# Routing of the first six batches inside the attention, fixed slot columns for each expert, and tables that pick the processed columns

## What is computed

```python
x = x + _L0_xattn_ref(_layernorm(x), ctx_2048, w_qkv, w_proj, b_proj)
x = x + _L0_ffn_ref(_layernorm(x), conf_w, conf_b, gate_w, up_w, down_w, wealth)
# _L0_ffn_ref, with x the normed rows:
confidences = jax.nn.sigmoid(jnp.einsum('bsh,eh->bse', x, conf_w) + conf_b)
bids = confidences * wealth
top_bids, selected_experts = jax.lax.top_k(bids, 2)
routing_weights = jax.nn.softmax(top_bids, axis=-1)
# per expert: down(silu(gate(x)) * up(x)), summed with the two weights
```

## Time and profile before

| | us |
|---|---|
| median of 3 runs (lowest to highest) | 543.18 (542.64 to 545.73) |
| the profiled execution's own time | 545.19 |
| its span, first to last instruction | 543.6 |

### The profile page before, as it was taken

One profiled execution on the slowest core, in us unless ns is written; L12 is line 12 of the kernel. 1 busy time (PEld: TensorE's weight loads), 2 busy tenths in 40 slices (PEclk: granted clock), 3 DMA queues, 4 the chain that ended last, 5 costly groups with the idle time before them and its releaser, 6 DMA issues. The chain is left out here.

```text
span 543.6 us, 10607 instructions
## 1 busy us (share of the span) xinstructions
PE 468.6 (86%) x3467; PEld 283.5 (52%) x3468; DVE 356.5 (66%) x646; ACT 290.1 (53%) x584; POOL 181.4 (33%) x381
## 2 busy tenths in 40 slices
PE   2489999999999999999999984736699999999930
PEld 1245555555555555555555532735266666666620
DVE  7798797887887987978898805478133333333317
ACT  2237877777877878777788783210033333333310
POOL 6141222412312313223101001014356766677630
PEclk9759999999999999999999998555599999999985
DMA  6512223343342333331212002500101111111126
GB/s 178 126 41 66 67 81 112 78 114 98 84 128 74 99 111 81 86 88 40 75 39 76 2 2 69 164 0 0 25 25 45 39 39 40 39 41 41 39 72 181
DMA packets 32254, 38.10 MB, mean 70 GB/s; under 512 B 5604, under 2 KB 20580, under 8 KB 32212
## 3 DMA queue, kind: packets, MB, share of 16 engines
q1 hardware_dynamic: 27252, 30.79, 21.0%
q0 software_dynamic: 2560, 5.25, 3.8%
q10 hardware_dynamic: 2400, 1.51, 1.0%
HBM read 16.58 MB, written 4.72 MB: 39 GB/s over the span
## 5 line engine op out<-in xcount | busy, mean ns | idle before, releaser
L463 DVE TENSOR_REDUCE max_part<-max_ps 128x2 f32<-128x1024 f32 (+1 forms) x192 | 225.9, 1220 | 38.5 <-PE max_ps L561 30.6
L422 ACT ACTIVATE probs<-ring_ps 128x512 f32<-128x512 f32 x384 | 198.4, 604 | 50.1 <-PE ring_ps L584 47.0
L584 PE MATMUL ring_ps<-blocks,keys 64*128 64x512 f32 x384 | 151.1, 471 | 2.1 <-ACT probs L422 1.7
L594 PE MATMUL pv_ps<-probs,value_cols 128*32 128x256 f32 x1536 | 103.4, 387 | 0.0
L561 PE MATMUL max_ps<-keys,blocks 64*128 64x512 f32 x256 | 84.6, 449 | 7.6 <-DMA blocks<-masked 6.5
L1018 DVE TENSOR_TENSOR hidden<-up_ps,silu 128x512 f32<-128x512 f32 x40 | 27.7, 692 | 84.1 <-PE up_ps L1108 81.9
L584 PEld LDWEIGHTS ring_ps<-blocks,keys 64*128 64x128 f32 x384 | 65.3, 186 | 31.9 <-ACT probs L422 25.5
L911 ACT ACTIVATE hiddenT<-at_ps 128x512 f32<-128x512 f32 x40 | 23.9, 597 | 75.7 <-PE at_ps L1125 67.2
L338 POOL CAST maxes<-rowmax 128x8 fp32r<-128x8 f32 x32 | 6.3, 197 | 170.3 <-DVE rowmax L470 170.3
L594 PEld LDWEIGHTS pv_ps<-probs,value_cols 128*32 128x32 f32 x1536 | 40.4, 109 | 40.3 <-issue 14.6
L561 PEld LDWEIGHTS max_ps<-keys,blocks 64*128 64x128 f32 x256 | 42.4, 196 | 26.8 <-issue 16.7
(11 more groups left out here) (148 smaller groups left out, 465.2 us busy)
## 6 DMA issues: line engine op xcount, KB each, us to landing
keys<-parts SPq DMA_DIRECT2D x96, 96.0 KB
blocks<-masked SPq DMA_DIRECT2D x93, 64.0 KB
ctx_v_sb<-ctx_v_dram SPq DMA_DIRECT2D x8, 256.0 KB, 2.9
gate<-gateT_dram SPq DMA_DIRECT2D x8, 256.0 KB, 2.9
up<-upT_dram SPq DMA_DIRECT2D x8, 256.0 KB, 2.9
y_in<-pick_outs SPq DMA_DIRECT2D x8, 256.0 KB, 5.0
raw<-ctx_kT_dram SPq DMA_DIRECT2D x7, 256.0 KB, 2.7
h_rows<-h SPq DMA_DIRECT2D x4, 256.0 KB, 5.2
```

Of the source, the lines that this page charges most:

```text
L422: act.activation(probs[par][:, k, PAIR * a:PAIR * (a + 1)], bank("exp", s * XUNITS + u)[:].rearrange("p (g n) -> p g n", n=N), ACT.Exp).th ...
L463: vec.reduce_max(out, bank, axis=AX.X).then_inc(max_done, 1)
L584: pe.matmul(ps[:], keys[rows, t, k * P:(k + 1) * P], blocks[rows, t], start=True, stop=True)\
L594: mm = pe.matmul(pv_ps[ROWS * g:ROWS * (g + 1), 0:N], value_cols[:, t, k, g, :], probs[q % 2][:, k, g, :], start=(k == 0), stop=(k == KT - 1))
```

## The change

**Within the attention.** DVE takes the statistics of batch b-1 in step r = 1 of batch b (`row_statistics`). POOL norms its rows in r = 2 (`norm_rows`, with a power instead of a root), SP stores them to DRAM in r = 3, and POOL forms the logits of one tile in each of the steps r = 0 and r = 1 of the next batch (`logits`: one product of 128 x 1024 and a tree of seven additions). So twelve tiles (EARLY) have logits by step 30. In step 30 DVE forms bids and ranks of these twelve (`early_bids`, `rank_tiles`), PE counts (`count_tiles`), and in steps 31 to 33 DVE computes their places and one-hot matrices (now 128 wide on both sides) in portions of 14, 5 and 5, and PE multiplies them in portions of 8 (`find`). POOL forms the logits of tiles 12 and 13 in the last steps.

**After the barrier.** Norms and logits are left for the last two tiles, ranks, places and one-hot matrices for the last four.

**Fixed columns.** Expert e owns the slot columns 16e to 16e+15, so a place needs no count of the other experts. Which 40 of the columns are processed stands in two tables that POOL computes, `table` (the expert) and `columns`. In the loop POOL reads the column number with a load into a register before each copy. The number of slots stays 40. `max_ps` (attention), `gate_ps` and `up_ps` (experts) share the PSUM tensors `wide`.

```diff
+EARLY = QT * (B - 2)
+REACH = TILES
+LAST = QUADS - 1
+HOT_TURNS = (0, 14, 19, 2 * EARLY)
...
+def rank_tiles(vec, r, lo, hi, pair, pair2):
...
+    pairs = [P, n, E, E]
+    this, other = bids.unsqueeze(3).to_broadcast(pairs), bids.unsqueeze(2).to_broadcast(pairs)
+    vec.tensor_tensor(pair2, other, this, ALU.is_gt)
+    then(vec.tensor_tensor(pair, other, this, ALU.is_equal))
+    then(vec.tensor_tensor(pair, pair, r.earlier[:].unsqueeze(1).to_broadcast(pairs), ALU.mult))
+    then(vec.tensor_tensor(pair, pair, pair2, ALU.add))
+    then(vec.tensor_reduce(rank, pair, axis=AX.X, op=ALU.add))
+    vec.tensor_scalar(r.picks[:, lo:hi, :], rank, 1.5, None, ALU.is_lt).then_inc(r.picks_ready, 1)
+    for k in range(2):
+        op = vec.tensor_scalar(top[:, k], rank, float(k), None, ALU.is_equal)
+    then(op)
+    for k in range(2):
+        op = vec.tensor_tensor(picked[:, k], top[:, k], bids, ALU.mult)
+    then(op)
+    then(vec.tensor_reduce(best[:, :, :, 0], picked, axis=AX.X, op=ALU.add))
+    for k in range(2):
+        vec.tensor_tensor(r.gap[:, k, lo:hi], best[:, k], best[:, 1 - k], ALU.subtract).then_inc(r.gap_ready, 1)
...
+def place_tiles(vec, r, lo, hi, ps, base):
...
+    n = hi - lo
+    place, top, picked = r.place[:, lo:hi], r.top[:, :, lo:hi], r.picked[:, :, lo:hi]
+    then(vec.tensor_tensor(place, ps[:, 0:n * E].rearrange("p (t e) -> p t e", e=E),
+                           base[:].unsqueeze(1).to_broadcast([P, n, E]), ALU.add))
+    for k in range(2):
+        op = vec.tensor_tensor(picked[:, k], top[:, k], place, ALU.mult)
+    then(op)
...
+def hot_pick(vec, r, k, t, lane_hot, slot_hot):
+
+    vec.tensor_scalar(lane_hot, r.index[:], r.lane[:, k, t:t + 1], r.pick_id[:, k * TILES + t:k * TILES + t + 1],
+                      ALU.is_equal, ALU.mult)
+    vec.tensor_scalar(slot_hot, r.index[:], r.slot[:, k, t:t + 1], None, ALU.is_equal).then_inc(r.hot_ready, 1)
...
+def count_tiles(pe, r, lo, hi, ps):
+
+    n = hi - lo
+    pe.matmul(ps[:, 0:(n + 1) * E], r.before_r[:], r.picks[:, lo:hi + 1].rearrange("p t e -> p (t e)"), start=True, stop=False)
+    for t in range(n):
+        mm = pe.matmul(ps[:, (t + 1) * E:(n + 1) * E], r.ones_r[:],
+                       r.picks[:, lo + t, :].unsqueeze(1).to_broadcast([P, n - t, E]), start=False, stop=(t == n - 1))
+    mm.then_inc(r.place_filled, 1)
...
+            def norm_rows(c):
+                rows = slice(QT * c, QT * (c + 1))
+                pool.wait_ge(aggr2_in, QT * (c + 1))
+                pool.tensor_scalar(router.var[:, rows], router.aggr[:, rows, 1], EPS, None, ALU.add).then_inc(var_in, 1)
+                pool.wait_ge(var_in, c + 1)
+                pool.tensor_tensor(router.rstd[:, 1, rows], router.var[:, rows], router.minus_half[:].to_broadcast([P, QT]), ALU.pow)\
+                    .then_inc(rstd2_in, 1)
+                pool.wait_ge(rstd2_in, c + 1)
+                for t in range(QT * c, QT * (c + 1)):
+                    pool.tensor_scalar(router.h[:, t, :], m.x[:, t, :], router.aggr[:, t, 0:1], router.rstd[:, 1, t:t + 1],
...
+            def logits(t):
+                pool.wait_ge(router.norm_out, t + 1)
+                pool.wait_ge(conf_in, 64)
+                wait_for(pool, router.z_ready, t)
+                pool.tensor_tensor(router.product[:], router.h[:, t, :].unsqueeze(1).to_broadcast([P, E, C]), router.conf_w[:], ALU.mult)\
+                    .then_inc(logit_done, 1)
+                width = C
+                for n in range(1, C.bit_length()):
+                    width //= 2
+                    pool.wait_ge(logit_done, C.bit_length() * t + n)
+                    pool.tensor_tensor(router.product[:, :, 0:width], router.product[:, :, 0:width], router.product[:, :, width:2 * width],
+                                       ALU.add).then_inc(logit_done, 1)
+                pool.wait_ge(logit_done, C.bit_length() * (t + 1))
+                pool.tensor_tensor(router.z[:, t, :], router.product[:, :, 0], router.conf_rows[:, 0], ALU.add).then_inc(router.z_ready, 1)
...
+                if r < QT and 2 <= b < B:
+                    logits(QT * (b - 2) + r)
...
+                if r == 2 and 1 <= b < B:
+                    norm_rows(b - 1)
+                if s == LAST:
+                    for t in range(QT):
+                        logits(QT * (b - 1) + t)
...
+                if s == LAST - 1:
+                    act.wait_ge(router.z_ready, EARLY)
+                    act.activation(ez[:], router.z[:, 0:EARLY], ACT.Exp, scale=-1.0).then_inc(ez_done, 1)
...
+            def row_statistics(c):
+                vec.wait_ge(proj_done, c + 1)
+                for i in range(QT * c, QT * (c + 1)):
+                    vec.bn_stats(router.stats[:, i, :], m.x[:, i, :]).then_inc(stats2_in, 1)
+                for i in range(QT * c, QT * (c + 1)):
+                    vec.wait_ge(stats2_in, i + 1)
+                    vec.bn_aggr(router.aggr[:, i, :], router.stats[:, i, :]).then_inc(aggr2_in, 1)
...
+            def early_hots(s):
+                first, last = HOT_TURNS[s - LAST:s - LAST + 2]
+                for t in range(T):
+                    vec.wait_ge(rows_in[t], rows_spread(QUADS - T + t))
+                for n in range(first, last):
+                    if n >= HOTS:
+                        vec.wait_ge(router.early_found, (n - HOTS) // 8 + 1)
+                    k, t = early_picks[n]
+                    hot_pick(vec, router, k, t, *hot_of(n))
...
                            .then_inc(proj_done, 1)
+                        row_statistics(b - 1)
                     if w == 1 and r == 0 and 0 <= b < B - 2:
                         normalize_x(b + 2)
+                    if w == 0 and s == LAST - 1:
+                        early_bids()
+                        rank_tiles(vec, router, 0, EARLY, *pair_early)
+                    if w == 3 and s > LAST:
+                        early_hots(s)
                     if w == 3 and 1 <= s <= QUADS:
                         normalize(s - 1)
+                    if w == 3 and s == LAST:
+                        vec.wait_ge(router.place_filled, 1)
+                        early_count = router.place_ps[0][:, EARLY * E:(EARLY + 1) * E]
+                        vec.tensor_tensor(router.late_row[:], early_count, router.expert_row[:], ALU.add)
+                        vec.tensor_scalar(router.rounded[:], early_count[0:1], float(P - 1), None, ALU.add)
+                        place_tiles(vec, router, 0, EARLY, router.place_ps[0], router.expert_row)
+                        early_hots(s)
...
+            def find(first, last):
+                for n in range(first, last):
+                    pe.wait_ge(router.hot_ready, n + 1)
+                    lane_hot, slot_hot = hot_of(n)
+                    mm = pe.matmul(router.found_ps, lane_hot, slot_hot, start=(n == 0), stop=False)
+                mm.then_inc(router.early_found, 1)
...
+                        if s == LAST - 1:
+                            pe.wait_ge(router.picks_ready, 1)
+                            pe.wait_ge(masks_ready, MASKS)
+                            pe.wait_ge(max_done, QUADS * MUNITS)
+                            count_tiles(pe, router, 0, EARLY, router.place_ps[0])
+                        if s == LAST:
+                            find(0, 8)
+                    if i == 3 and s == QUADS:
+                        find(8, 16)
+                    if i == 1 and s == QUADS + 1:
+                        find(16, 2 * EARLY)
...
+            then(pool.tensor_copy(end[:, 0], tiles_of[:]))
+            pool.tensor_scalar(room[:], tiles_of[:], -1.0, float(REACH), ALU.mult, ALU.add)
+            for n, by in enumerate((1, 2, 4)):
+                pool.tensor_copy(end[:, n + 1, 0:by], end[:, n, 0:by])
+                then(pool.tensor_tensor(end[:, n + 1, by:E], end[:, n, by:E], end[:, n, 0:E - by], ALU.add))
+            then(pool.tensor_tensor(beyond, router.slot_index[:].unsqueeze(2).to_broadcast(by_slot), over_slots(end[:, 3]),
+                                    ALU.subtract))
+            then(pool.tensor_scalar(beyond, beyond, 0.0, None, ALU.is_ge))
+            then(pool.tensor_tensor(roomy, beyond, over_slots(room[:]), ALU.mult))
+            for by in (4, 2, 1):
+                then(pool.tensor_tensor(both[:, :, :, 0:by], both[:, :, :, 0:by], both[:, :, :, by:2 * by], ALU.add))
+            then(pool.tensor_scalar(both[:, 0, :, 1], both[:, 0, :, 0], float(E - 1), None, ALU.min))
+            pool.tensor_copy(table[:], both[:, 0, :, 1]).then_inc(table_ready, 1)
+            then(pool.tensor_tensor(both[:, 1, :, 1], both[:, 1, :, 0], router.slot_index[:], ALU.add))
+            then(pool.tensor_copy(columns[:], both[:, 1, :, 1]))
+            pool.wait_ge(router.h_stored, 16 * B)
             pool.wait_ge(sources_ready, 2)
...
+            def column_of(j):
+                return bass.ds(pool.value_load(columns[0:1, bass.ds(j, 1)], min_val=0, max_val=COLUMNS - 1), 1)
...
```

(8 more changed lines are left out.)

399 lines of the change are left out of this document (188 added, 211 removed).

## The result

| | before | changed |
|---|---|---|
| median, us | 544.39 (4 runs) | 561.17 (4 runs) |
| ratio | 1 | 1.0315 (1.0283 to 1.0348) |
| profiled: time / span | 545.19 / 543.6 | 561.55 / 559.9 |
| PE clock, mean | 0.912 | 0.916 |

What follows compares the result with a forecast made beforehand. PE bounds the attention's steady part, nobody the router; in the loop PE is 96% busy. 545.2 - 25.6 (router) + 14 (last steps) + 8 (steady part) + 15 (loop) = 556.6, 555 against the median; range 532 to 576.

Steps and rivals of the forecast that it cites:

- The loop: Expert slots: two register loads between copied y and load of x add 0.42 us a slot, 15 us (0 to 33).
- The slack: Loop: spare time between issue of the load of x and PE's use, between 0 and 1.1 us, taken as 0.55.
- The rival on which the sign hung: Loop does not feel the loads and DVE is hardly held: 537 us as a median, faster; chance 0.22.
- the one that POOL's queue can't run ahead across a load: Loop: both loads add to POOL's own cycle, 4.4 us a slot, 47 added in place of 15: 587; chance 0.1.
- The third, a slipping attention: Attention: POOL's logits don't fit into r = 0 and r = 1, PE waits at its transposes: 573 us; chance 0.13.
- The steady part: Attention before the last steps: row statistics 2 us and DVE norms held by POOL 6 us, 8 added (2 to 18).
- The hold of a pair of norms: Step r = 0: POOL's product lengthens DVE's two norms by 1.75 us, 1.5 net in each of four batches.
- The last steps: End of the attention: ranking, counting, places and one-hots of the early tiles add 14 us (8 to 19).
- Quad 29: Step 30: ranking ahead of quad 29's normalizing delays it by 2.0 us, plus 2.0 for sharing with POOL: 4.0.
- Quad 29 to 30: Last steps: 13 counting matmuls put into PE's list, 1.0 us exposed.
- Quad 30 to 31: Last steps: places and one-hots delay PE's first find by 3.5 us; one-hots ahead of the last normalizing add 2.5.
- The router: Stretch from barrier to first gate matmul: 51.1 us falls to 25.5, saving 25.6 (21 to 28).

Runs made afterwards that it cites:

- Run 1: Kernel before the change, with two unused register loads added per slot on POOL, one ahead of each copy: 1.0287, 560 us.
- run 2: Changed kernel with both column loads of a slot moved ahead of POOL's waits for the transposed x and copied y: 1.0101, 550 us.
- Run 3: Changed kernel with DVE's two norms in step r = 0 behind the fifth of six reductions instead of the second: 1.0259, 558.5 us.
- run 5: Changed kernel with POOL's logits of tiles 12 and 13 held back until DVE has ranked the first twelve tiles: 1.0239, 557 us.
- Run 6: Changed kernel with 21 idle matmuls in PE's step 30, ahead of the exp matmuls waiting for quad 29's normalizing: 1.0236, 557 us.
- Run 7: Changed kernel with early one-hot pairs respread, twelve of them behind the barrier, and PE's finds behind the last transposes: 1.0281, 560 us.
- run 4: Changed kernel with the twelve-tile ranking behind quad 29's normalizing and PE's counting behind quad 30's transposes: 1.0193, 555 us.
- run 8: Changed kernel with the edits of run 2, Run 3, run 4, run 5 and Run 7 together, measured twice: 0.9830 and 0.9810, 535 and 534 us.

## Why the prediction was right, and where it was not

**The loop, +15 forecast, +14.7 measured: right, by its own steps.** From the copied y to the issue the two loads added 1.16 (2.17 less 1.01), where 1.3 was taken. The slack was taken as 0.55 in the middle of 0 and 1.1; 1.16 / 2 is 0.58 a slot without any slack, and the slots from the sixth on grew by 0.44. So there was some 0.3 of slack for two slots, and the rest of the term came out of a slightly long load and a slightly large slack together; the 0.05 put down for PE's own load can't be told apart from them. Run 1 shows the cause. The rival on which the sign hung, that the slack of x hides the loads (537), falls with it. So does the one that POOL's queue can't run ahead across a load (587): in run 2 it does, and that is the remedy. The third, a slipping attention (573), falls by the steps: all but four keep their length.

The Trainium skill's "DMA: Bandwidth & Descriptors", § Latency and other measured facts, has a floor of about 600 ns under a register load. On POOL TENSOR_LOAD is 0.29, and the whole group with the register operations, seen between the two copies, 0.66; the floor agrees only if it means the group. With it as the price of the load alone the loop would have grown by 26, and it didn't.

**The steady part, +8 forecast, +3.7 measured.** The mechanism was right, two sizes were off. The hold of a pair of norms was put at 1.75, from the start of the kernel; it is 1.99 less 0.61, 1.4, of which 0.85 reached the row maxima. The row statistics were put at 2 and cost nothing: in these steps the row maxima keep their distance. Run 3 shows that nothing else is in it.

**The last steps, +14 forecast, +21.3 measured: the step that failed.** By its parts:

- Quad 29: 4.0 forecast, 5.3 measured. The ranking with its bids ran from 316.40 to 327.17, 10.8 us. The forecast had 7.3 and 2.0 for sharing. POOL held five short instructions by 2.7 (run 5), 0.7 more than the 2.0, and the ranking's own 8.1 are 0.8 more than the 7.3 (the reciprocal of the bids alone is 0.76, not one of the short ones).
- Quad 29 to 30: 1.0 forecast for the counting, 6.6 measured. Here the prediction had no term for the clock. It counted every instruction at the clock of 1.00 of the earlier trace rows, while the wait that it forecast itself, 4.0 for quad 29, was long enough to lose it: in run 5 2.58 us were enough. Run 6 gives 3.2 of the 6.6 back by keeping PE busy, and the twelve counting matmuls alone take 2.68 in place of 1.46. Even at 1.00 the counting is 1.6 (329.22 to 330.83 in run 6), not 1.0, which leaves some 5.0 for the clock; that part is an estimate.
- Quad 30 to 31: 6.0 forecast (3.5 and 2.5), 6.6 measured. Run 7 shows it to be the one-hots and finds.
- From there to the barrier: 3.0 forecast, 2.8 measured.

**The router, 25.5 left forecast, 27.3 measured** (29.6 less the 2.3 of one-hots counted above): to cut 51.1 in half was right. The tables were to end last. They end at 376.8, and DVE's `source`, whose one-hots were held beside them, 0.3 later at 377.16; POOL's first column load starts at 377.28. Of the 1.8 by which the stretch is longer than forecast 1.5 had gone before the tables began (at 368.72, 10.0 behind the statistics without the 2.3, where 8.5 was forecast). The loads ahead of the four first copies stand 0.66 apart, as taken:

```profile
373.45 1.98 POOL L1056 TENSOR_TENSOR both<-both 1x320 f32<-1x320 f32 x3
...
376.58 0.24 POOL L1060 CAST columns<-both 1x40 int32<-1x40 f32 x1
376.93 0.23 DVE L1168 TENSOR_SCALAR source<-token 128x128 uint32<-128x128 f32 x1
...
378.24 0.19 POOL L1097 COPY source_now<-source 128x1 uint32 x1 [1.42 <-issue]
378.90 0.18 POOL L1097 COPY source_now<-source 128x1 uint32 x1 [0.48 <-issue]
```

The forecast was 4 too high in the steady part and 7 and 2 too low in these two, so that it stood only 6 below the result has some luck in it (1.2 of the 6 is the median of the kernel before, 543.18 when the sum was made and 544.39 now). The sign has none: of 23.8 saved behind the statistics 21.3 went in the last steps, and the 2.5 that stay can't pay for the loop.

## What to carry to other kernels

Work that is moved from a stretch where the engines wait into one where they seem idle is paid at each hand-over there: count what stands behind it on its engine's list, and let the result that the bounding engine waits for go first (runs 4 and 7, in their traces: the same work, 7 and 3 us less). A register load belongs ahead of the wait, not behind it: two loads behind one cost 0.44 us a slot, the same two ahead of it next to nothing. Where two engines hold each other, the order of arrival says which one pays, so the short instruction on the path should not come behind the other's long one. And a change that loses as a whole is to be taken apart before it is dropped: no edit here was worth the whole loss, yet five of them turned 3.2% slower into 1.7 to 1.9% faster, and with the logits of two tiles moved to PE in place of edit 5 it is 2.5%.

## What the runs showed of the hardware

- POOL's TENSOR_TENSOR holds DVE's one-input float32 instructions on SBUF until it is through, up to 2.18 us for one of 0.34, and the short pair of L128 with two inputs by 0.55 (0.98 in place of 0.43). DVE's wide ones with two inputs (L118 to L121, 0.96 alone) took at most 1.10 beside POOL (run 4), but they had begun first or nearly so, and then POOL was held: additions of 0.21 to 0.32 took 0.85 to 0.92, norms of 0.80 took 2.03 and 1.12, a product of 2.36 took 2.70. Beside DVE's reductions, which read PSUM, POOL's products stayed at 2.34 to 2.39. So the prediction's remark on the four pair instructions was right that they stand against POOL's additions; it was POOL that waited. "GPSIMD Engine Reference", § 1 Specifications, of the Trainium skill names two kinds as contended, DVE's two-port modes and instructions with two SBUF inputs. The holds of the two-input ones agree with it; in which mode the one-input ones ran no trace here shows.
- A wait of 5.4 us on PE was followed by some 15 us at 1.2 GHz, although PE was busy for 94% of them. Waits of 4.59 (run 2) and 2.58 us (run 5) lost the clock too; filled with idle matmuls, the same wait left it at 1.00 for 5 us more. A wait is not needed for a fall: in the last steps of run 8 no gap of PE ahead of it was above 0.52 us, and the clock was 0.50 from 330.0 to 333.4 in one execution and 1.00 in the other. What decides that, and when it comes back (near 343 in the change, at 336.5 in run 2, at 386 in run 5), isn't settled.
- POOL's queue does run ahead of its engine, register loads included, as far as the next wait (run 2).
- Left open: why four of the five executions of run 2 took 5 us longer than the profiled one.
